# One-hots of a graph kernel's first pass built slot by slot: a single-source compare with a per-partition number in place of a two-tensor compare

## The chip, the cores and the metric

The kernel runs on one core of a Trainium2 chip. The metric is the device time of one execution in microseconds, the median over runs. The engines are named as in the profile: PE (matrix products), PEld (its weight loads), DVE (the vector engine), ACT (the scalar engine), POOL (GpSimd, which issues the row gathers here) and SP (which issues most other DMAs).

## What the reference computes

`x` holds 6250 rows of 256 numbers, `src` and `dst` the ends of 206250 edges, `edge_type_500` a type in 0..499 for each edge. Four layers follow one another, each added to `x` after a layer norm. Cut to what matters:

```python
# layer 1 (3125 nodes and 50000 edges in the original; here 6250 and 206250)
t1  = feat @ W1
msg = t1[src] + feat[src] * feat[dst] @ W2
msg = msg / (sqrt(out_deg[src]) * sqrt(out_deg[dst]))[:, None]
agg = segment_sum(msg, dst)                 # rows of edges added up per dst node
embed = where(in_cnt > 0, t1 + agg, 0) + b  # leaky_relu, then unit norm
# layer 2
x = x + layernorm(x) @ weight.T + bias
# layer 3
m = clifford_linear(h[src] * relation_emb[edge_type], msg_w, msg_b)
m = m * sigmoid(relation_emb[edge_type] @ gate_w.T + gate_b) * norm(deg[src] * deg[dst])
x = x + clifford_linear(h + segment_sum(m, dst), upd_w, upd_b)
# layer 4: gelu feed-forward of the top-k rows by a score, scaled by it
```

The edges come sorted by `dst` (there is a slow path for those that are not, which is not taken here). The kernel uses that order to cut them into windows.

## The kernel before, in words

The 6250 nodes are 49 blocks (`NB`) of 128 (`P`). Each block has 35 (`C`) tiles of 128 edge slots. The program has four stages by time:

* a prelude (to some 290 us): counts, block and window boundaries, degrees, the gate of the relations, and the table `t1_d`, also kept in three bf16 parts in SBUF (`parts_t`);
* the first pass (to some 1670 us), layers 1 and 2, with the sort of each block's edges by type;
* the second pass, layer 3, with layer 4's products beside it: gathers of 1715 tiles on POOL (L834), products on DVE (L1854), sums on PE (L958);
* the top-k and the output.

**The first pass.** It is written out by hand, step by step: every engine has a loop over the same step number `t`, 16 steps (`WINS`) to a block, with what it has to do at each step. The order on an engine is therefore fixed, and semaphores join the engines. Blocks are summed in two ways. Odd blocks gather their edges' source rows on POOL (L886, 24 blocks of 35 tiles) and sum them by one-hots (`sel1`, built by DVE at L1832) on PE at L1012. Even blocks have a count matrix instead: for each window of 8 destination nodes PE multiplies a one-hot of the source's low 7 bits (`hot_l`, 3 tiles of 128) with a one-hot of the source's block and the destination's node (`hot_r`, 392 + 294 + 147 = 833 columns for the three tiles of a window), at L985. ACT copies the counts out (L1421), and PE multiplies them with the table in three bf16 parts (L998).

DVE builds these one-hots in `edge_hots(n)`, two windows (`TWO`) at a time, 200 calls (`BATCHES`), one every four steps. The tiles hold the two windows interleaved, innermost: `hot_r` is `(n t)`, `hot_l` is `(c n t)`, and `ramp` holds 0, 0, 1, 1, 2, 2, .... A call is three compares of two tensors for `hot_r` (784, 588 and 294 elements per partition, L1818) and one for `hot_l` (768, L1821). The keys are the edges' numbers, turned to partitions by PE and copied out of PSUM to float16 by `window_keys` (L1807 and L1808).

The sort: for each block and each third of its 35 tiles (12, 12, 11), `sends(b, g)` builds `to_s` (L1943), three scaled copies `to_s3` (L1946) and `to_q`, the one-hot of the target's partition (L1948, 12 tiles of 128 in one compare of two tensors, 1536 elements). PE multiplies them at L1040 (`move`), three steps later in its own order. There is one buffer of each, so `sends` of the next third first waits for `s_sm`, PE's signal that it has read the last. `spot_q`, the targets, is written in float16 at L1930, once per three blocks. `edge_hots` has two buffers and waits for `s_h`, the histogram before last.

DVE's order in a step is: `features`, `pick_rows` (L1832), `edge_hots`, `sends`, the windows' bits and keys, `marks`, `loads3`, `totals`, `places`, then the small steps of the layer norms, each with its waits. `link(...)` is a DVE instruction on whose own completion DVE waits. Neither `edge_hots` nor the last compare of `sends` has such a link.

Of the kernel before, what the change touches and what calls it, by code (L numbers as in the profile page):

```python
# [13 lines left out]
P = 128  # L14
# [5 lines left out]
NB = -(-N // P)  # L20
# [6 lines left out]
C = 35  # L27
# [124 lines left out]
def program(nc, x, src, dst, etype, w1_0, w2_0, b_0, wf, bf, rel, msg_w, msg_b, upd_w, upd_b,  # L152
            gate_w, gate_b, wr, br, w1, b1, w2, b2, out):
    ctx = ExitStack()
    with ctx:
# [40 lines left out]
        ramp = arena[:, o:o + NODES * NB].bitcast(F16).rearrange("p (n t) -> p n t", t=TWO)  # L196
        o += NODES * NB
# [65 lines left out]
        word = arena[:, o:o + RW].bitcast(I32)  # L263
        o += RW + 1
# [4 lines left out]
        keyed_lo = arena[:, o:o + TAKE * WINS].bitcast(F16).rearrange("p (h q c w) -> p h q c w", h=2, c=TAKE, w=FOUR)  # L269
        o += TAKE * WINS  # L270
        keyed_hi = arena[:, o:o + TAKE * WINS].bitcast(F16).rearrange("p (h q c w) -> p h q c w", h=2, c=TAKE, w=FOUR)
        o += TAKE * WINS
# [22 lines left out]
        spot_q = Xf[:, o:o + RB * (C + 1)].bitcast(F16).rearrange("p (r b k) -> p r b k", r=2, k=C + 1)  # L295
        o += RB * (C + 1)
# [3 lines left out]
        to_q = Xf[:, o:o + TC4 * P // 2].bitcast(F16).rearrange("p (g q t) -> p g q t", q=P, t=TWO)  # L300
# [15 lines left out]
        hot_r = [t[:, 0:half_r].bitcast(BF16).rearrange("p (n t) -> p n t", t=TWO) for t in hots]  # L316
        hot_l = [t[:, half_r:half_r + half_l].bitcast(BF16).rearrange("p (c n t) -> p c n t", c=TAKE, t=TWO) for t in hots]
# [492 lines left out]
        def _(pool):  # L810
# [11 lines left out]
            pool.iota(ramp, [[1, NODES * NB], [0, TWO]], base=0, channel_multiplier=0,  # L822
# [72 lines left out]
        def _(pe):  # L895
            pe.wait_ge(s_const, 12)
# [444 lines left out]
        def _(act):  # L1341
# [16 lines left out]
            act.wait_ge(s_const, 12)  # L1358
# [254 lines left out]
        def _(dve):  # L1613
# [20 lines left out]
            dve.wait_ge(s_const, 12)  # L1634
# [167 lines left out]
            def window_keys(b):  # L1802

                dve.wait_ge(s_wtp, b + 1)
                lo = psE[:, 2, 0:TAKE * WINS].rearrange("p (q w c) -> p q c w", w=FOUR, c=TAKE)
                hi = psE[:, 2, TAKE * WINS:2 * TAKE * WINS].rearrange("p (q w c) -> p q c w", w=FOUR, c=TAKE)
                v.tensor_copy(keyed_lo[:, b % 2, :, :, :], lo)  # L1807
                link(v.tensor_scalar(keyed_hi[:, b % 2, :, :, :], hi, 2000.0, -2000.0, ALU.min, ALU.max))  # L1808
# [102 lines left out]
            def places(r, i):  # L1911

                b, nb = RB * r + i, blocks_of(r)
                m, first = BINS * C, C * i
                dve.wait_ge(s_rp, 2 * b + 2)
                flat = before[:, 0:m]
                mine = marked[:, i, :, :].rearrange("p c k -> p (c k)")
                link(v.tensor_tensor(flat, flat, psT[:, 0, 0:m], ALU.add))
                dve.sem_inc(s_pl, 1)
                link(v.tensor_tensor(flat, flat, mine, ALU.mult))  # L1920
                link(v.tensor_reduce(spot[:, first:first + C], flat.rearrange("p (c k) -> p k c", k=C), AX, ALU.add))
                link(v.memset(before[:, 0:1], 0.0))
# [7 lines left out]
                v.tensor_copy(spot_q[:, r % 2, 0:nb, 0:C], three(src_b[:, 0:w]))  # L1930
                link(v.tensor_copy(spot_s[:, r % 2, 0:nb, 0:C], three(src_a[:, 0:w])))

            def sends(b, g):

                n, r, i = THIRDS * b + g, b // RB, b % RB
                if n >= 1:
# [5 lines left out]
                count = lambda n: ramp[:, 0:n, :].unsqueeze(1).broadcast_to([P, m, n, TWO])  # L1942
                link(v.tensor_tensor(to_s, two(spot_s[:, r % 2, i, some]).broadcast_to([P, m, C, TWO]), count(C),  # L1943
                                     ALU.is_equal))
                for j in range(3):
                    v.tensor_tensor(to_s3[:, :, j, :, :], to_s,  # L1946
                                    two(load3[:, r % 2, j, i, some]).broadcast_to([P, m, C, TWO]), ALU.mult)
                v.tensor_tensor(to_q, two(spot_q[:, r % 2, i, some]).broadcast_to([P, m, P, TWO]),  # L1948
                                count(P), ALU.is_equal).then_inc(s_tq, 1)

            def first_pass():
                dve.wait_ge(s_part, NB)
                for t in (spot_q, spot_s):
                    v.memset(t[:, :, :, C:C + 1], 0.0)
# [343 lines left out]
```

## Time and profile before

| what | value |
|---|---|
| time, median of 3 runs | 3934.56 us (3927.07 to 3935.37) |
| span of the profiled execution | 3930.4 us |
| busy in the span: PE, DVE, POOL, ACT | 3456.7, 2831.5, 2610.6, 944.3 us |
| first pass, 325 to 1600 us: PE, DVE, POOL, ACT busy | 1193.5, 1177.6, 937.4, 483.5 us of 1275 |

The profiled execution has no time of its own in the results beside its span. It lies 4.2 us under the median and within the spread of the three runs.

Two DVE instructions with no wait between them overlap: the profile gives each its duration from start to completion, and the next starts some 0.08 us before the end of the last. What an instruction costs the engine is the distance from its start to the next one's start. It is read from the timeline, where a row with "xN" has N instructions, its start is that of the first, and its length reaches to the last one's end. Busy time counts overlapped time once. A row's shape is that of the first instruction in it.

### The profile page before, as it was taken

How to read it: one execution, taken by the hardware profiler on the slowest of the kernel's cores; microseconds unless marked ns; L12 is line 12 of the kernel's file. 1: busy time of each engine (PE TensorE's matmuls, PEld its weight loads, DVE VectorE, ACT ScalarE, POOL GpSimd, SP SyncE). 2: the span in 40 equal slices, each digit the busy share in tenths (PEclk: the TensorE clock that was granted, in tenths of full speed). 3: DMA queues.
4: the chain of work that ended last, by engine and by line, in shares of the span. 5: the costliest groups of instructions: out<-in, count | busy, mean ns of one | idle time of the engine just before them, and what ended most of it. 6: DMA issues, size and time to landing. Idle time of an engine off the chain costs nothing.

```text
span 3930.4 us, 69081 instructions
## 1 busy us (share of the span) xinstructions
PE 3456.7 (88%) x22700; PEld 2702.4 (69%) x22700; DVE 2831.5 (72%) x9160; ACT 944.3 (24%) x2408; POOL 2610.6 (66%) x2573
## 2 busy tenths in 40 slices
PE   6827999999999999778999999999999999999995
PEld 6825777777777777646776777777767777677764
DVE  8989999999999999555556556556565556656555
ACT  4042333333333434300111111111111111111111
POOL 1002777777777777367777777777777777777770
PEclk7557999999999999889999999999999999999998
DMA  5221443433443434275555555555555545555542
GB/s 154 69 88 34 111 108 108 114 107 108 109 111 106 113 107 110 81 216 135 137 135 135 135 135 136 137 135 135 136 137 134 136 133 139 136 135 133 139 129 75
DMA packets 261937, 478.46 MB, mean 122 GB/s; under 512 B 78704, under 2 KB 179072, under 8 KB 261588
## 3 DMA queue, kind: packets, MB, share of 16 engines
q0 software_dynamic: 122640, 340.29, 33.3%
q1 hardware_dynamic: 119412, 116.75, 10.2%
q10 hardware_dynamic: 19536, 17.02, 1.4%
q8 instruction: 189, 3.10, 0.3%
q14 instruction: 160, 1.31, 0.1%
HBM read 438.84 MB, written 35.00 MB: 121 GB/s over the span
## 4 chain that ended last, share of the span: by engine, by line
PE 32%; DVE 30%; POOL 20%; issue 10%; DMA 5%; ACT 2%; DVEq 0%; SPq 0%; POOLq 0%; ACTq 0%
POOL arena L834 20%; PE psE L958 6%; DMA arena<-t_d,srci 4%; PE psE L998 4%; PE psE L1012 4%; DVE relw L1818 3%; PE psE L1232 3%; DVE arena L1793 3%; DVE X L1832 2%; DVE arena L1711 2%; DVE X L1946 2%; PE psY L943 2%; PE psT L943 2%; DVE X L1948 2%; PE psE L1213 2%
## 5 line engine op out<-in xcount | busy, mean ns | idle before, releaser
L834 POOL DMA_INDIRECT arena<-t_d,srci x1715 | 1634.3, 953 | 582.2 <-issue 556.6
L886 POOL DMA_INDIRECT X<-t_d,srci x840 | 964.1, 1148 | 645.5 <-issue 450.0
L958 PE MATMUL psE<-arena 128*128 128x257 f32 x3430 | 1068.7, 393 | 79.0 <-DVE arena L1854 75.8
L1854 DVE TENSOR_TENSOR arena<-arena,psY 128x257 f32<-128x257 f32 x857 | 349.8, 420 | 437.2 <-DMA arena<-t_d,srci 235.9
L1854 DVE TENSOR_TENSOR arena<-arena,psT 128x257 f32<-128x257 f32 x858 | 349.9, 420 | 421.4 <-DMA arena<-t_d,srci 219.1
L958 PEld LDWEIGHTS psE<-arena 128*128 128x128 f32 x3430 | 541.5, 194 | 160.8 <-DVE arena L1854 84.5
L998 PE MATMUL psE<-arena,X 128*128 128x256 bf16 (+1 forms) x3675 | 535.9, 276 | 0.0
L1012 PE MATMUL psE<-X 128*128 128x257 f32 x1680 | 486.8, 383 | 8.2 <-DVE X L1832 7.7
L943 PE MATMUL psT<-relw,arena 126*128 126x257 bf16 x2574 | 434.3, 277 | 13.1 <-DVE arena L1845 13.1
L943 PE MATMUL psY<-relw,arena 126*128 126x257 bf16 x2577 | 433.1, 277 | 0.0
L998 PEld LDWEIGHTS psE<-arena,X 128*128 128x128 bf16 x3675 | 350.3, 99 | 81.6 <-issue 0.8
L1793 DVE TENSOR_SCALAR arena<-iof,dstf 128x128 f32<-128x128 f32 x1715 | 365.6, 297 | 2.9 <-PE psE L958 2.4
L943 PEld LDWEIGHTS psT<-relw,arena 126*128 126x128 bf16 x2574 | 253.2, 98 | 160.6 <-DVE arena L1845 13.7
L943 PEld LDWEIGHTS psY<-relw,arena 126*128 126x128 bf16 x2577 | 253.4, 98 | 146.5 <-issue 6.8
L1012 PEld LDWEIGHTS psE<-X 128*128 128x128 f32 x1680 | 265.0, 192 | 27.4 <-DVE X L1832 10.8
L1818 DVE TENSOR_TENSOR relw<-arena 128x784 bf16<-128x784 f16 (+2 forms) x600 | 231.3, 439 | 0.8
L1213 PE MATMUL psE<-arena 128*128 128x256 f32 (+1 forms) x800 | 189.0, 381 | 9.7 <-DVE rstd L2057 7.3
L1832 DVE TENSOR_SCALAR X<-iof,dstf 128x128 f32<-128x128 f32 x840 | 183.9, 294 | 0.9
L921 PE MATMUL psY<-arena 125*128 125x49 bf16 x1650 | 158.8, 269 | 20.8 <-DVE arena L1711 20.1
L1213 PEld LDWEIGHTS psE<-arena 128*128 128x128 f32 x800 | 145.4, 192 | 35.6 <-DVE rstd L2057 15.5
L921 PEld LDWEIGHTS psY<-arena 125*128 125x128 bf16 x1650 | 147.9, 143 | 31.6 <-DVE arena L1711 31.6
L1711 DVE TENSOR_TENSOR arena<-arena 125x3840 bf16<-125x3840 bf16 x110 | 162.5, 1536 | 3.9 <-PE psY L921 2.3
(346 smaller groups left out, 4423.1 us busy)
## 6 DMA issues: line engine op xcount, KB each, us to landing
arena<-types_d SPq DMA_DIRECT2D x245, 220.5 KB
arena<-t_d,srci POOLq DMA_INDIRECT x1715, 3.0
X<-t_d,srci POOLq DMA_INDIRECT x840
arena<-acc_d SPq DMA_DIRECT2D x98, 130.0 KB
arena<-dst_p SPq DMA_DIRECT2D x400, 1.5 KB
arena<-src_p SPq DMA_DIRECT2D x400, 1.5 KB
acc_d<-arena ACTq DMA_DIRECT2D x1, 6370.0 KB, 22.5
t_d<-arena SPq DMA_DIRECT2D x7, 910.0 KB, 4.3
```

Source lines behind the costliest of these rows:

```text
L834: pool.indirect_dma_start(gath[:, n % RG, :], None, t2_d, bass.IndirectOffsetOnAxis(ap=srci[:, n:n + 1], axis=0)).then_inc(s_g[n % RG], 16)
L886: pool.indirect_dma_start(ring1[:, n % RG1, :], None, t1_d, bass.IndirectOffsetOnAxis(ap=srci[:, at:at + 1], axis=0)).then_inc(s_g[n % RG1 ...
L921: ins = nc.tensor.matmul(psY[:, 0, 0:NB], ohlo[:, n % 2, :, t], ohhi[:, n % 2, :, t], start=(n == t == 0), stop=(n == HN - 1 and t == HG - 1))
L943: ins = nc.tensor.matmul(psR[n % BANKS][:, 0:DW], oht[0:PT, g % 2, at, :], relb[0:PT, part, c, 0:DW], start=((c, part) == (mine[0][0], 0)) ...
L958: ins = nc.tensor.matmul(psE[:, b % 2, 0:DW], sel[:, n // SG % 3, k % SG, :], gath[:, n % RG, 0:DW], start=False, stop=(k == C - 1))
L998: ins = nc.tensor.matmul(bank[:, 0:wide], adj[:, i % 2, s, :], parts_t[:, s, at0:at0 + wide], start=(s == part == 0), stop=(s == NB - 1 an ...
L1012: ins = nc.tensor.matmul(psE[:, 1, 0:DW], sel1[:, n // SG1 % 2, k % SG1, :], ring1[:, n % RG1, 0:DW], start=(k == 0), stop=(k == C - 1))
L1213: ins = nc.tensor.matmul(bank[:, i * D:i * D + many * P].rearrange("p (q n) -> p q n", n=P), f1[:, t, ht * P:ht * P + P], rows[:, t, :, :] ...
L1793: ins = v.tensor_scalar(sel[:, n % 3, i, :], iof[:, :], dstf[:, k + i:k + i + 1], None, ALU.is_equal)
L1818: v.tensor_tensor(hot_r[n % 2][:, AT[c]:AT[c + 1], :], keyed_hi[:, b % 2, j, c, first:first + TWO].unsqueeze(1).broadcast_to([P, many, TWO ...
L1832: ins = v.tensor_scalar(sel1[:, n % 2, j, :], iof[:, :], dstf[:, k + j:k + j + 1], None, ALU.is_equal)
L1854: v.tensor_tensor(rows, rows, psR[n % BANKS][:, 0:DW], ALU.mult).then_inc(s_po, 1)
```

## The change

Every one-hot of `edge_hots` and of `to_q` is now made by a compare of one tensor (the ramp, now without pairs) with a number per partition that is read from memory as float32, one instruction for each tile of 128 edges. The layouts follow: `hot_r` is `(t n)`, `hot_l` is `(t c n)`, `to_q` is `(k q)`, so that PE reads them without a stride. `keyed_lo`, `keyed_hi` and `spot_q` are float32. `to_s` still is a compare of two tensors, with a small ramp of pairs of its own (`pairs_to`), for which there is one more constant to wait for. `spot_q` and `word` have changed places in memory. A call of `edge_hots` is now 12 instructions (6 of 128 elements, 2 each of 392, 294 and 147), a block's `to_q` 35 of 128.

```diff
-        ramp = arena[:, o:o + NODES * NB].bitcast(F16).rearrange("p (n t) -> p n t", t=TWO)
+        ramp = arena[:, o:o + NODES * NB // 2].bitcast(F16)
+        pairs_to = arena[:, o:o + C + 1].bitcast(F16).rearrange("p (n t) -> p n t", t=TWO)
...
-        to_q = Xf[:, o:o + TC4 * P // 2].bitcast(F16).rearrange("p (g q t) -> p g q t", q=P, t=TWO)
+        to_q = Xf[:, o:o + TC4 * P // 2].bitcast(F16).rearrange("p (k q) -> p k q", q=P)
...
-        hot_r = [t[:, 0:half_r].bitcast(BF16).rearrange("p (n t) -> p n t", t=TWO) for t in hots]
-        hot_l = [t[:, half_r:half_r + half_l].bitcast(BF16).rearrange("p (c n t) -> p c n t", c=TAKE, t=TWO) for t in hots]
+        hot_r = [t[:, 0:half_r].bitcast(BF16).rearrange("p (t n) -> p t n", t=TWO) for t in hots]
+        hot_l = [t[:, half_r:half_r + half_l].bitcast(BF16).rearrange("p (t c n) -> p t c n", t=TWO, c=TAKE) for t in hots]
...
             def edge_hots(n):
-                b, j, first = n * TWO // WINS, n * TWO % WINS // FOUR, n * TWO % FOUR
+                b = n * TWO // WINS
                 if n >= 2:
                     dve.wait_ge(s_h, TWO * (n - 1))
-                for c, (lo, hi) in enumerate(REACH):
-                    many = (hi - lo) * NB
-                    v.tensor_tensor(hot_r[n % 2][:, AT[c]:AT[c + 1], :],
-                                    keyed_hi[:, b % 2, j, c, first:first + TWO].unsqueeze(1).broadcast_to([P, many, TWO]),
-                                    ramp[:, lo * NB:hi * NB, :], ALU.is_equal)
-                v.tensor_tensor(hot_l[n % 2][:, :, :, :],
-                                keyed_lo[:, b % 2, j, :, first:first + TWO].unsqueeze(2).broadcast_to([P, TAKE, P, TWO]),
-                                ramp[:, 0:P, :].unsqueeze(1).broadcast_to([P, TAKE, P, TWO]), ALU.is_equal).then_inc(s_r, 1)
+                for t in range(TWO):
+                    w = (n * TWO + t) % WINS
+                    for c, (lo, hi) in enumerate(REACH):
+                        v.tensor_scalar(hot_r[n % 2][:, t, AT[c]:AT[c + 1]], ramp[:, lo * NB:hi * NB],
+                                        keyed_hi[:, b % 2, w, c:c + 1], None, ALU.is_equal)
+                        ins = v.tensor_scalar(hot_l[n % 2][:, t, c, :], ramp[:, 0:P], keyed_lo[:, b % 2, w, c:c + 1], None,
+                                              ALU.is_equal)
+                ins.then_inc(s_r, 1)
...
-                v.tensor_tensor(to_q, two(spot_q[:, r % 2, i, some]).broadcast_to([P, m, P, TWO]),
-                                count(P), ALU.is_equal).then_inc(s_tq, 1)
+                for k in third(g):
+                    ins = v.tensor_scalar(to_q[:, k % TC4, :], ramp[:, 0:P], spot_q[:, r % 2, i, k:k + 1], None, ALU.is_equal)
+                ins.then_inc(s_tq, 1)
```

On DVE, early in the first pass, the order before has one call of `edge_hots` (L1818 and L1821), one of `sends` (L1943 to L1948) and the next call's start. `relw` holds the one-hots of counts, `X` those of the sort, `arena` the ramp and the keys.

```order
L1818 TENSOR_TENSOR relw<-arena 128x784
L1818 TENSOR_TENSOR relw<-arena 128x588
L1818 TENSOR_TENSOR relw<-arena 128x294
L1821 TENSOR_TENSOR relw<-arena 128x768
L1943 TENSOR_TENSOR X<-relw,arena 128x420
L1946 TENSOR_TENSOR X<-X 128x6x70 x3
L1948 TENSOR_TENSOR X<-X,arena 128x1536
```

Now the second window's half of such a call, and the same `sends` behind it; the first window's half is the same six rows once more ahead of these.

```order
L1823 TENSOR_SCALAR relw<-arena 128x392
L1825 TENSOR_SCALAR relw<-arena 128x128
L1823 TENSOR_SCALAR relw<-arena 128x294
L1825 TENSOR_SCALAR relw<-arena 128x128
L1823 TENSOR_SCALAR relw<-arena 128x147
L1825 TENSOR_SCALAR relw<-arena 128x128
L1946 TENSOR_TENSOR X<-relw,arena 128x420
L1949 TENSOR_TENSOR X<-X 128x6x70 x3
L1952 TENSOR_SCALAR X<-arena 128x128 x12
```

Nothing has changed places: four instructions have become twelve at each call, and the one of `to_q` has become twelve (eleven in a block's last third).

## Rows read from the trace of the kernel before

**Rows 1.** The page, part 1: busy us, share, instructions of each engine.
```profile
PE 3456.7 (88%) x22700; PEld 2702.4 (69%) x22700; DVE 2831.5 (72%) x9160; ACT 944.3 (24%) x2408; POOL 2610.6 (66%) x2573
```

**Rows 2.** Windows by engine: length, busy us (instructions), clock share, DMA, GB/s.
```profile
35.00:225.00 190.00, 162.40 (x1667) 150.93 (x1666) 181.12 (x169) 51.05 (x207) 0.00 (x0) 0.52 0.30 79
325.00:1600.00 1275.00, 1193.49 (x9014) 942.92 (x9013) 1177.60 (x3902) 483.53 (x1350) 937.37 (x812) 0.98 0.39 106
1600.00:1680.00 80.00, 55.29 (x312) 42.11 (x309) 34.46 (x126) 25.23 (x79) 17.09 (x18) 0.82 0.23 65
```

**Rows 3.** Waits from 325 to 1600 us: total us, times, longest us.
```profile
POOL X L886 <- PE psE L1012: 189.7, 229, 67.0
PE psY L1040 <- DVE X L1948: 41.7, 19, 3.8
PE psE L1096 <- DVE arena L2077: 16.2, 23, 1.1
DVE arena L2034 <- PE psE L998: 15.6, 9, 2.8
DVE arena L2034 <- PE psE L1012: 10.7, 9, 1.7
PE psT L985 <- DVE relw L1821: 9.9, 17, 0.8
DVE X L1943 <- PE psY L1040: 3.8, 3, 1.9
DVE arena L1918 <- PE psT L1030: 1.0, 1, 1.0
```

**Rows 4.** Timeline of DVE near 903 us: start us, length us, instructions.
```profile
901.47 0.95 DVE L1948 TENSOR_TENSOR X<-X,arena 128x1536 f16<-128x1536 f16 x1
902.34 1.06 DVE L1832 TENSOR_SCALAR X<-iof,dstf 128x128 f32<-128x128 f32 x5
903.32 1.16 DVE L1818 TENSOR_TENSOR relw<-arena 128x784 bf16<-128x784 f16 x3
904.39 0.55 DVE L1821 TENSOR_TENSOR relw<-arena 128x768 bf16<-128x768 f16 x1
904.86 0.15 DVE L2083 RECIPROCAL rstd<-rstd 128x1 f32<-128x1 f32 x1
```

**Rows 5.** DVE groups by shape, whole span: busy us, mean ns, idle before.
```profile
L1948 DVE TENSOR_TENSOR X<-X,arena 128x1536 f16<-128x1536 f16 x147 | 139.8, 951 | 0.0
L1818 DVE TENSOR_TENSOR relw<-arena 128x784 bf16<-128x784 f16 x200 | 111.7, 559 | 0.8
L1821 DVE TENSOR_TENSOR relw<-arena 128x768 bf16<-128x768 f16 x200 | 110.1, 551 | 0.0
L1818 DVE TENSOR_TENSOR relw<-arena 128x294 bf16<-128x294 f16 x200 | 60.8, 304 | 0.0
L1845 DVE TENSOR_SCALAR arena<-arena,tid 126x896 bf16<-126x896 f16 x49 | 23.0, 470 | 0.0
L1845 DVE TENSOR_SCALAR arena<-arena,tid 126x128 bf16<-126x128 f16 x52 | 13.7, 267 | 0.0
```

**Rows 6.** Timeline of DVE near 2188 us; L1845 here is 512, then 128 wide.
```profile
2188.05 0.58 DVE L1845 TENSOR_SCALAR arena<-arena,tid 126x512 bf16<-126x512 f16 x2
2188.47 0.67 DVE L1793 TENSOR_SCALAR arena<-iof,dstf 128x128 f32<-128x128 f32 x3
```

**Rows 7.** POOL's groups on the page, part 5: the gathers of both passes.
```profile
L834 POOL DMA_INDIRECT arena<-t_d,srci x1715 | 1634.3, 953 | 582.2 <-issue 556.6
L886 POOL DMA_INDIRECT X<-t_d,srci x840 | 964.1, 1148 | 645.5 <-issue 450.0
```

**Rows 8.** Timeline of the first microseconds: constants on POOL, first compare on DVE.
```profile
7.92 4.38 POOL L822 IOTA arena<- 128x784 f16 x1
13.33 0.25 DVE L1637 TENSOR_SCALAR arena<-arena 125x110 int32<-125x110 int32 x1 [10.82 <-DMA arena<-in_dst]
```

**Rows 9.** Groups of the first pass whose output the change retypes, whole span.
```profile
L1807 DVE CAST arena<-psE 128x48 f16<-128x48 f32 x25 | 5.0, 200 | 0.0
L1808 DVE TENSOR_SCALAR arena<-psE 128x48 f16<-128x48 f32 x25 | 4.9, 196 | 0.0
L1930 DVE CAST X<-arena 128x105 f16<-128x105 int32 x16 | 4.2, 265 | 0.5
```

**Rows 10.** PE's histogram and the plain products of the first pass.
```profile
L985 PE MATMUL psY<-relw 128*128 128x392 bf16 x60 | 20.4, 340 | 0.0
L998 PE MATMUL psE<-arena,X 128*128 128x257 bf16 x363 | 99.8, 275 | 0.0
L1040 PEld LDWEIGHTS psY<-X 128*128 128x128 f16 x525 | 30.7, 100 | 20.8 <-DVE X L1948 16.1
L998 PEld LDWEIGHTS psE<-arena,X 128*128 128x128 bf16 x1090 | 103.3, 99 | 23.4
```

More of the change, by code:

```diff
@@ L195, in program @@
         o = -(-(NB * TW // 2) // 2) * 2
-        ramp = arena[:, o:o + NODES * NB].bitcast(F16).rearrange("p (n t) -> p n t", t=TWO)
-        o += NODES * NB
+        ramp = arena[:, o:o + NODES * NB // 2].bitcast(F16)
+        o += NODES * NB // 2
+        pairs_to = arena[:, o:o + C + 1].bitcast(F16).rearrange("p (n t) -> p n t", t=TWO)
+        o += C + 1
         start_w = arena[:, o:o + STEPS].bitcast(I32)
@@ L262, in program @@
         o += 2 * RW
-        word = arena[:, o:o + RW].bitcast(I32)
-        o += RW + 1
+        spot_q = arena[:, o:o + 2 * RW].rearrange("p (r b k) -> p r b k", r=2, k=C)
+        o += 2 * RW + 1
         types_h = arena[:, o:o + P].bitcast(F16).rearrange("p (r e) -> p r e", r=2)
@@ L268, in program @@
         o += PAIRS * NB + 1
[L269 to L272, printed above, removed]
+        keyed_lo = arena[:, o:o + 2 * TAKE * WINS].rearrange("p (h w c) -> p h w c", h=2, c=TAKE)
+        o += 2 * TAKE * WINS
+        keyed_hi = arena[:, o:o + 2 * TAKE * WINS].rearrange("p (h w c) -> p h w c", h=2, c=TAKE)
+        o += 2 * TAKE * WINS
         marked = arena[:, o:o + BINS * RW // 2].bitcast(BF16).rearrange("p (b c k) -> p b c k", b=RB, c=BINS)
@@ L294, in program @@
         o += 2 * SG1 * P
-        spot_q = Xf[:, o:o + RB * (C + 1)].bitcast(F16).rearrange("p (r b k) -> p r b k", r=2, k=C + 1)
-        o += RB * (C + 1)
+        word = Xf[:, o:o + RW].bitcast(I32)
+        o += RW
         load3 = Xf[:, o:o + 3 * RB * (C + 1)].bitcast(F16).rearrange("p (r j b k) -> p r j b k", r=2, j=3, k=C + 1)
@@ L821, in _ @@
             pool.iota(offset, [[-NODES, WINS]], base=0, channel_multiplier=1, allow_small_or_imprecise_dtypes=True).then_inc(s_const, 1)
-            pool.iota(ramp, [[1, NODES * NB], [0, TWO]], base=0, channel_multiplier=0,
+            pool.iota(ramp, [[1, NODES * NB]], base=0, channel_multiplier=0,
+                      allow_small_or_imprecise_dtypes=True).then_inc(s_const, 1)
+            pool.iota(pairs_to, [[1, C + 1], [0, TWO]], base=0, channel_multiplier=0,
                       allow_small_or_imprecise_dtypes=True).then_inc(s_const, 1)
@@ L895, in _ @@
         def _(pe):
-            pe.wait_ge(s_const, 12)
+            pe.wait_ge(s_const, 13)
             for n in range(EN):
@@ L984, in histogram @@
                 for c, (lo, hi) in enumerate(REACH):
-                    ins = nc.tensor.matmul(bank[:, lo * NB:hi * NB], hot_l[n % 2][:, c, :, j],
-                                           hot_r[n % 2][:, AT[c]:AT[c + 1], j], start=(c == 0), stop=(c == TAKE - 1))
+                    ins = nc.tensor.matmul(bank[:, lo * NB:hi * NB], hot_l[n % 2][:, j, c, :],
+                                           hot_r[n % 2][:, j, AT[c]:AT[c + 1]], start=(c == 0), stop=(c == TAKE - 1))
                 ins.then_inc(s_h, 1)
@@ L1039, in move @@
                     i, t = k % TC4 // TWO, k % TWO
-                    ins = nc.tensor.matmul(psY[:, 0, 0:3 * C], to_q[:, i, :, t], to_s3[:, i, :, :, t],
+                    ins = nc.tensor.matmul(psY[:, 0, 0:3 * C], to_q[:, k % TC4, :], to_s3[:, i, :, :, t],
                                            start=(k == 0), stop=(k == C - 1))
@@ L1631, in _ @@
             link(v.memset(end_hi, -1.0))
-            dve.wait_ge(s_const, 12)
+            dve.wait_ge(s_const, 13)
             dve.wait_ge(s_dst, 32)
@@ L1804, in window_keys @@
                 dve.wait_ge(s_wtp, b + 1)
[L1805 to L1808, printed above, removed]
+                lo = psE[:, 2, 0:TAKE * WINS].rearrange("p (w c) -> p w c", c=TAKE)
+                hi = psE[:, 2, TAKE * WINS:2 * TAKE * WINS].rearrange("p (w c) -> p w c", c=TAKE)
+                v.tensor_copy(keyed_lo[:, b % 2, :, :], lo)
+                link(v.tensor_copy(keyed_hi[:, b % 2, :, :], hi))
                 dve.sem_inc(s_key, 1)
             def edge_hots(n):
[L1813 removed]
+                b = n * TWO // WINS
                 if n >= 2:
                     dve.wait_ge(s_h, TWO * (n - 1))
[L1816 to L1823 removed]
+                for t in range(TWO):
[6 more added lines that the diff above has]
+                ins.then_inc(s_r, 1)
             def pick_rows(n):
@@ L1929, in places @@
                 link(v.tensor_scalar(src_a[:, 0:w], src_a[:, 0:w], 7, None, ALU.logical_shift_right))
-                v.tensor_copy(spot_q[:, r % 2, 0:nb, 0:C], three(src_b[:, 0:w]))
+                v.tensor_copy(spot_q[:, r % 2, 0:nb, :], three(src_b[:, 0:w]))
                 link(v.tensor_copy(spot_s[:, r % 2, 0:nb, 0:C], three(src_a[:, 0:w])))
@@ L1941, in sends @@
                 two = lambda a: a.rearrange("p (g t) -> p g t", t=TWO).unsqueeze(2)
-                count = lambda n: ramp[:, 0:n, :].unsqueeze(1).broadcast_to([P, m, n, TWO])
-                link(v.tensor_tensor(to_s, two(spot_s[:, r % 2, i, some]).broadcast_to([P, m, C, TWO]), count(C),
-                                     ALU.is_equal))
+                link(v.tensor_tensor(to_s, two(spot_s[:, r % 2, i, some]).broadcast_to([P, m, C, TWO]),
+                                     pairs_to[:, 0:C, :].unsqueeze(1).broadcast_to([P, m, C, TWO]), ALU.is_equal))
                 for j in range(3):
@@ L1947, in sends @@
                                     two(load3[:, r % 2, j, i, some]).broadcast_to([P, m, C, TWO]), ALU.mult)
-                v.tensor_tensor(to_q, two(spot_q[:, r % 2, i, some]).broadcast_to([P, m, P, TWO]),
-                                count(P), ALU.is_equal).then_inc(s_tq, 1)
+                for k in third(g):
+                    ins = v.tensor_scalar(to_q[:, k % TC4, :], ramp[:, 0:P], spot_q[:, r % 2, i, k:k + 1], None, ALU.is_equal)
+                ins.then_inc(s_tq, 1)
             def first_pass():
                 dve.wait_ge(s_part, NB)
-                for t in (spot_q, spot_s):
-                    v.memset(t[:, :, :, C:C + 1], 0.0)
+                v.memset(spot_s[:, :, :, C:C + 1], 0.0)
                 v.memset(load3[:, :, :, :, C:C + 1], 0.0)
```

2 lines of the change are left out of this document (1 added, 1 removed).

## The prediction
> **What bounds the kernel now.** The page's busy shares come first [rows 1]: PE 88%, DVE 72%, POOL 66%. They are averages over stages, so the next view is the windows by engine. The change touches only the first pass. In its steady part, 325 to 1600 us, PE is busy 1193.5 and DVE 1177.6 of 1275 us, POOL 937.4 [rows 2]. Both PE and DVE look full, and what decides is who waits for whom there [rows 3]. DVE waits for PE in four rows: 15.6 + 10.7 + 3.8 + 1.0 = 31 us. DVE's other idle time, 97 - 31 = 66 us, is its own: it waits for the completion of its linked instructions, which a busy PE does not explain and a faster PE would not remove. PE waits for DVE longer (41.7 + 16.2 + 9.9 in the three rows shown), nearly all of its 81.5 us of idle time. So DVE sets the pace, with PE close behind. The rule for the sum follows: DVE's order is fixed by hand, so each us added to it lengthens the pass, less at most the 31 us in which it stands waiting for PE.
>
> **What an instruction costs DVE.** The timeline gives start to start [rows 4]. The three L1818 take 904.39 - 903.32 = 1.07 us and L1821 0.47 us, so a call of edge_hots is 1.54 us. L1948 takes 902.34 - 901.47 = 0.87 us, 0.08 under its duration of 951 ns [rows 5]. The rate of the two-tensor form is (559 - 304) / (784 - 294) = 0.52 ns per element [rows 5], and its fixed part 559 - 83 - 784 x 0.52 = 68 ns.
>
> The new form is not in the first pass, but the second pass has it: L1845 compares a float16 tile with a float32 number per partition and writes bf16. Its rate is (470 - 267) / (896 - 128) = 0.264 ns per element [rows 5], half of the other's. Its fixed part is larger. The pair of 512 and 128 elements takes 2188.47 - 2188.05 = 0.42 us [rows 6], so 2f + 640 x 0.264 = 420 and f = 126 ns. The float32 form L1832 agrees: five in 0.98 us is 196 ns each [rows 4], and 128 elements at twice 0.264 leave 128 ns. I take 127 ns, which makes 128, 147, 294 and 392 elements 161, 166, 205 and 230 ns. This is the center of the argument. The rate halves, but a number per partition costs some 60 ns more per instruction, and there are many more instructions.
>
> The Trainium skill speaks for the change on the rate: VectorE: DVE Perf Modes, "The perf-mode tier table", has 16-bit tensor_scalar at 4 elements a cycle and tensor_tensor at 2. The rates 0.264 and 0.52 agree. The same page of the Trainium skill, in "The TRN2 errata", prices an instruction at 58 cycles plus elements over the mode's width at 0.96 GHz. By that a 128-wide compare would be 94 ns, a call of edge_hots 1.36 for 1.51 us, a block's to_q 3.28 for 2.51, and the whole change +7 us. The rows do not bear this out: they have 161 ns, and 196 where the float32 form would be 127.
>
> **The change part by part.**
>
> * edge_hots, 200 calls. Removed: 1.54 us. Added: 2 x (230 + 205 + 166 + 3 x 161) = 2.17 us. That is +0.63 us a call and +125 us in all.
> * to_q, 49 blocks. Removed: 3 x 0.87 = 2.61 us. Added: 35 x 161 = 5.64 us. That is +3.03 us a block and +148 us in all.
> * Collisions with POOL. L1832's compares run beside POOL's gathers and still start 196 ns apart [rows 4]; the pair at L1845 gives the same fixed part within 2 ns. From no delay to 10 ns on each of 2400 + 1715 = 4115 instructions it is +0 to +41 us. I take +12, 3 ns each, nearest to the rows.
> * PE's waits give back. DVE's 31 us of waiting for PE can go, but those at L2034 are for sums that end right before them and remain in part. I take -15, between 0 and -31.
> * Retyped outputs: L1807 and L1808 write 48 elements from PSUM, L1930 105 elements, in 265 ns or less [rows 9], with the same counts per partition. The clamp of L1808 becomes a copy. One memset less. At 25 and 16 times this is under 1 us either way, and I count 0.
> * PE's reads without a stride. L985 at 392 columns takes 340 ns with its pairs interleaved, L998 at 257 contiguous columns 275 ns [rows 10]. The difference is 65 ns for 135 columns, 0.48 ns each, which is one column per cycle at 2.4 GHz and a little. Weight loads are 100 and 99 ns. The stride costs nothing now, so nothing comes back: 0.
> * The ramp: POOL's iota of 784 elements ends at 12.3 us and halves, but DVE's first compare waits for the DMA of dst until 13.3 [rows 8]: 0.
> * The added constant wait is for an iota of 72 elements in the same place, behind the same DMA: 0.
> * In the second pass nothing changes.
>
> Sum: 125 + 148 + 12 - 15 = +270 us on the profiled span of 3930.4, which is 4200. The runs' median is 4 us above that span, well inside what the terms are good for. **I predict 4200 us**, 6.8% slower. The pass would then have DVE busy in about 1450 of 1545 us and PE in 1193.5, or 77%.
>
> POOL does not become late. It issues 840 gathers at 1148 ns [rows 7], 964 us in a pass that grows by 270, and it waits 189.7 us for PE's release already [rows 3]. Even at 1.5 us a gather it would be 1260 of some 1600 us.
>
> **The rivals.**
>
> * *The one-hots off even offsets run at half rate.* A window's hot_r has 833 columns, an odd number of 2-byte elements, so the second window's tiles start 2 bytes off a word. The third tile reads the ramp from column 245, odd too. That concerns 147 + 392 + 294 + 147 = 980 of a call's 2434 elements. At L1818's rate of 0.52 they cost 0.26 us a call more, +52 us: 4252. At half that rate again it would be +155 us: 4355. Against it no row of this trace speaks, since all its 16-bit tiles start even; for it neither. The Trainium skill has the rule against this rival: Vector Engine (DVE) Microarchitecture Reference, "Performance modes", says that 4-byte alignment makes no difference. No run here shows it yet. Chance 10%.
> * *PE takes the gap badly.* With PE at 77% the granted clock can fall to the lower of its levels, 1.2 for 2.4 GHz. The rows have 0.98 at 94% busy, 0.82 at 69% in 1600 to 1680 us, and 0.52 in the prelude, where PE waits for DVE in turns [rows 2]. At a clock share of 0.85 PE's work would be 1193.5 x 0.98 / 0.85 = 1376 us, still under 1545, so most of it hides. What shows is where DVE waits for sums, L2034 and the chain of layers 1 and 2. If the 31 us of waits double instead of halving, that is +46 on my sum: 4246. Chance 8%.
> * *Not slower.* The fixed part of the new form could be smaller in this place, where twelve independent compares follow one another, than at L1845 and L1832. Without the number's 60 ns, at the 68 ns of L1818, the 4115 instructions would cost 4115 x 59 = 243 us less: 3957. The break-even of the four parts lies at 127 - 270 / 4115 us = 61 ns; under that the kernel is not slower. For it: nothing in the rows, and twelve in a row are no different from L1832's five, which already run at 196 ns. Against it: two independent readings of 126 and 128 ns. By the Trainium skill's price above the time would be 3937, on this side or next to it. Chance 3%.
> * *PE, not DVE, was the limit*, so that DVE's extra time hides. PE's idle time is 81.5 us in the pass. Were all of it slack that DVE may fill, the gain would be cut to 270 - 82 = 188: 4118. The waits above speak against it, since PE's idle time is waiting for DVE. Chance 3%.
>
> That the change doesn't do what it says is excluded by the order: twelve single-source compares stand where four two-source ones stood.
>
> **How the numbers follow.** My forecast has 76%, the rivals 10, 8, 3 and 3. Within the forecast the ends are all of the 31 us given back and no collisions (3930 + 273 - 31 = 4172), and none given back with +41 (4244). I widen to the rivals at 4252 and 4246 with room for both together, and to the low side for an f of 120 ns (-29). Range 4145 to 4290. A change within 0.2% (8 us) is what the measurement can't tell from none. Slower by more 97.5%, same 1.5%, faster 1%.
>
> **What would show it.** L1952 (to_q) at a start-to-start distance of 0.16 us, twelve in 1.93 us. A call of edge_hots at 2.17 us, with its two halves 1.09 us each; a second half that is longer is the first rival. The pass's end moves from about 1670 to 1940 us, and the second pass keeps its length. DVE idle on PE in the pass under 31 us, PE waiting for DVE by some 300 us more, mostly at L1040's and L985's successors. A clock well under 0.98 there with DVE waiting more than before is the second rival. I am wrong if the compares start 0.12 us apart or less, or if DVE's total grows as said and the span doesn't.

## The result, and the profile after

| kernel | median us | runs | ratio to before, 95% interval |
|---|---|---|---|
| before | 3933.48 (3927.07 to 3935.37) | 4 | |
| changed | 4191.91 (4189.17 to 4199.80) | 4 | 1.066 (1.0647 to 1.0673) |

The changed kernel is slower by 258 us. The forecast was 4200 us, range 4145 to 4290. Its profiled execution took 4199.8 us with a span of 4197.8, the slowest of the four, so the profiled spans are 267 us apart and the medians 258.

The page's busy times of the changed kernel:

```profile
PE 3519.8 (84%) x22700; PEld 2724.1 (65%) x22700; DVE 3119.7 (74%) x12327; ACT 936.8 (22%) x2408; POOL 2473.5 (59%) x2574
```

DVE has 3167 instructions and 288 busy us more, PE the same 22700 matmuls [rows 1]. The windows by engine show where. The first two rows are the whole first pass of before, then of the changed kernel; the last two are the second pass and the tail of each.

```profile
300.00:1640.00 1340.00, 1244.21 (x9334) 980.67 (x9335) 1219.29 (x4043) 500.28 (x1397) 954.46 (x830) 0.97 0.38 104
```
```profile
300.00:1900.00 1600.00, 1310.28 (x9347) 1006.46 (x9347) 1509.95 (x7204) 494.08 (x1399) 816.49 (x830) 0.93 0.33 87
```
```profile
1680.00:3930.00 2250.00, 2009.73 (x11469) 1541.55 (x11469) 1330.78 (x4660) 332.18 (x639) 1634.29 (x1715) 0.97 0.51 137
```
```profile
1940.00:4190.00 2250.00, 2008.96 (x11469) 1538.60 (x11469) 1329.35 (x4658) 332.17 (x639) 1637.73 (x1715) 0.97 0.52 136
```

The busy times of the second pass and the tail are the same to 4 us on every engine; the loss is in the first pass. The second pass's first gather starts at 1680.71 us before and at 1939.21 us in the changed kernel, 258.5 us later. The other 9 us between the two profiled spans are in the second pass and the tail. In the first pass DVE's busy time grows by 1509.95 - 1219.29 = 291 us. The granted clock's share (1 is 2.4 GHz, 0.5 is 1.2 GHz) falls from 0.97 to 0.93, and POOL is busy 138 us less.

The timeline of DVE in the changed kernel (start us, length us), to be read against [rows 4]: one third's to_q, and a whole call of edge_hots.

```profile
1003.05 1.90 DVE L1952 TENSOR_SCALAR X<-arena 128x128 f16<-128x128 f16 x11
1004.88 0.14 DVE L2064 TENSOR_SCALAR ssq<-ssq 128x1 f32<-128x1 f32 x1
...
1005.65 0.32 DVE L1823 TENSOR_SCALAR relw<-arena 128x392 bf16<-128x392 f16 x1
1005.88 0.25 DVE L1825 TENSOR_SCALAR relw<-arena 128x128 bf16<-128x128 f16 x1
1006.04 0.29 DVE L1823 TENSOR_SCALAR relw<-arena 128x294 bf16<-128x294 f16 x1
1006.25 0.25 DVE L1825 TENSOR_SCALAR relw<-arena 128x128 bf16<-128x128 f16 x1
1006.41 0.40 DVE L1823 TENSOR_SCALAR relw<-arena 128x147 bf16<-128x147 f16 x1
1006.59 0.26 DVE L1825 TENSOR_SCALAR relw<-arena 128x128 bf16<-128x128 f16 x1
1006.76 0.30 DVE L1823 TENSOR_SCALAR relw<-arena 128x392 bf16<-128x392 f16 x1
1006.98 0.25 DVE L1825 TENSOR_SCALAR relw<-arena 128x128 bf16<-128x128 f16 x1
1007.14 0.30 DVE L1823 TENSOR_SCALAR relw<-arena 128x294 bf16<-128x294 f16 x1
1007.36 0.24 DVE L1825 TENSOR_SCALAR relw<-arena 128x128 bf16<-128x128 f16 x1
1007.52 0.25 DVE L1823 TENSOR_SCALAR relw<-arena 128x147 bf16<-128x147 f16 x1
1007.69 0.45 DVE L1825 TENSOR_SCALAR relw<-arena 128x128 bf16<-128x128 f16 x1
1007.85 0.72 DVE L1910 TENSOR_TENSOR_SCAN arena<-ones,psT 128x280 f32<-128x280 f32 x1
```

From start to start the 128-wide compares are 0.16 us apart, the 294-wide 0.21, the 392-wide 0.23. The call takes 1007.85 - 1005.65 = 2.20 us (2.17 expected, 1.54 before), and its second half 1.09 us, no longer than its first, 1.11. Eleven of to_q take 1.83 us (11 x 0.161 = 1.77 expected).

The waits of the changed kernel's first pass, 325 to 1860 us, against [rows 3]:

```profile
POOL X L890 <- PE psE L1016: 647.0, 433, 83.8
...
PE psY L1044 <- DVE X L1952: 173.6, 70, 5.3
...
PE psT L989 <- DVE relw L1825: 53.8, 46, 1.5
...
DVE arena L2052 <- PE psE L1100: 0.3, 1, 0.3
```

The last row is the only wait of DVE for PE that is left, 0.3 us in place of 31. PE now waits for the one-hots of the sort and of the counts.

### The profile page after: what moved, and what is told of

Read it like the earlier page. It is cut to its first block, busy times and chain, and to the rows that moved or that the text cites. A ratio compares the mean times of both kernels' runs of the same rounds, so it can differ in the third digit from the quotient of the medians.

```text
span 4197.8 us, 72249 instructions
## 1 busy us (share of the span) xinstructions
PE 3519.8 (84%) x22700; PEld 2724.1 (65%) x22700; DVE 3119.7 (74%) x12327; ACT 936.8 (22%) x2408; POOL 2473.5 (59%) x2574
## 4 chain that ended last, share of the span: by engine, by line
DVE 45%; POOL 20%; PE 18%; issue 10%; DMA 5%; ACT 1%; DVEq 0%; SPq 0%; POOLq 0%; ACTq 0%
POOL arena L838 20%; DVE X L1952 7%; DVE relw L1823 6%; PE psE L962 5%; DVE relw L1825 5%; DVE X L1836 4%; DMA arena<-t_d,srci 4%; DVE X L1949 3%; PE psE L1236 3%; DVE arena L1797 3%; DVE arena L1715 2%; PE psY L925 2%; PE psY L947 2%; PE psT L947 2%; DVE X L1946 1%
## 5 line engine op out<-in xcount | busy, mean ns | idle before, releaser
L890 POOL DMA_INDIRECT X<-t_d,srci x840 | 826.2, 984 | 1045.9 <-PE psE L1016 648.2
L962 PEld LDWEIGHTS psE<-arena 128*128 128x128 f32 x3430 | 538.2, 193 | 166.2 <-DVE arena L1858 91.3
L1002 PE MATMUL psE<-arena,X 128*128 128x256 bf16 (+1 forms) x3675 | 550.8, 281 | 0.0
L1016 PE MATMUL psE<-X 128*128 128x257 f32 x1680 | 508.2, 397 | 13.3 <-DVE X L1836 13.3
L1823 DVE TENSOR_SCALAR relw<-arena 128x392 bf16<-128x392 f16 (+2 forms) x1200 | 358.8, 300 | 0.8
L1825 DVE TENSOR_SCALAR relw<-arena 128x128 bf16<-128x128 f16 x1200 | 306.5, 256 | 0.0
L1016 PEld LDWEIGHTS psE<-X 128*128 128x128 f32 x1680 | 276.4, 199 | 37.7 <-DVE X L1836 19.2
L1952 DVE TENSOR_SCALAR X<-arena 128x128 f16<-128x128 f16 x1715 | 297.5, 269 | 0.0
L1044 PE MATMUL psY<-X 128*128 128x105 f16 x1715 | 121.7, 225 | 180.3 <-DVE X L1952 179.8
L1044 PEld LDWEIGHTS psY<-X 128*128 128x128 f16 x1715 | 102.3, 105 | 223.0 <-DVE X L1952 214.7
```

What stands on the lines that cost most here:

```text
L890: pool.indirect_dma_start(ring1[:, n % RG1, :], None, t1_d, bass.IndirectOffsetOnAxis(ap=srci[:, at:at + 1], axis=0)).then_inc(s_g[n % RG1 ...
L962: ins = nc.tensor.matmul(psE[:, b % 2, 0:DW], sel[:, n // SG % 3, k % SG, :], gath[:, n % RG, 0:DW], start=False, stop=(k == C - 1))
L1002: ins = nc.tensor.matmul(bank[:, 0:wide], adj[:, i % 2, s, :], parts_t[:, s, at0:at0 + wide], start=(s == part == 0), stop=(s == NB - 1 an ...
L1016: ins = nc.tensor.matmul(psE[:, 1, 0:DW], sel1[:, n // SG1 % 2, k % SG1, :], ring1[:, n % RG1, 0:DW], start=(k == 0), stop=(k == C - 1))
L1823: v.tensor_scalar(hot_r[n % 2][:, t, AT[c]:AT[c + 1]], ramp[:, lo * NB:hi * NB], keyed_hi[:, b % 2, w, c:c + 1], None, ALU.is_equal)
L1825: ins = v.tensor_scalar(hot_l[n % 2][:, t, c, :], ramp[:, 0:P], keyed_lo[:, b % 2, w, c:c + 1], None, ALU.is_equal)
```

## The experiments

The ratio is to the kernel before as it was timed together with the experiment: 3936.5 us for e1 to e4, 3934.35 for e5 to e8, 3936.87 for e9. Differences in the text are to that, or to the changed kernel's 4191.91. Those of e4, e5 and e9 are under 2% of the time, but their intervals lie clear of 1. The edits are cut to what matters.

| kernel | median us | ratio to before, 95% interval |
|---|---|---|
| e1_hots_only | 4046.53 | 1.0281 (1.0264 to 1.0298) |
| e2_toq_only | 4060.96 | 1.0321 (1.0303 to 1.0338) |
| e3_constant_keys | 4055.87 | 1.0305 (1.0288 to 1.0322) |
| e4_before_two_parts | 3904.17 | 0.9920 (0.9903 to 0.9936) |
| e5_sel1_two_tensor | 3911.49 | 0.9940 (0.9927 to 0.9954) |
| e6_after_two_parts | 4193.49 | 1.0657 (1.0641 to 1.0673) |
| e7_float_source | 4287.88 | 1.0898 (1.0882 to 1.0915) |
| e8_both_sel_two_tensor | 4034.74 | 1.0257 (1.0242 to 1.0271) |
| e9_sel_in_two | 3979.91 | 1.0110 (1.0094 to 1.0127) |

**The two halves alone.** e1 is the changed kernel with to_q as it was (with spot_q in float16 again, a longer ramp of pairs and PE's reads with a stride, not shown):

```diff
-                for k in third(g):
-                    ins = v.tensor_scalar(to_q[:, k % TC4, :], ramp[:, 0:P], spot_q[:, r % 2, i, k:k + 1], None, ALU.is_equal)
-                ins.then_inc(s_tq, 1)
+                v.tensor_tensor(to_q, two(spot_q[:, r % 2, i, some]).broadcast_to([P, m, P, TWO]),
+                                pairs_to[:, 0:P, :].unsqueeze(1).broadcast_to([P, m, P, TWO]), ALU.is_equal).then_inc(s_tq, 1)
```

> Only edge_hots is changed to twelve single-source compares; to_q stays one compare of two tensors. Theory (DVE paces the first pass and every added us of it counts): 200 calls x 0.63 us = +125 us, less some 10 us of DVE's waits for PE: 4045 to 4060 us. Rival (PE's 82 us of idle time absorb DVE's first extra time): +45 to +80 us, 3980 to 4015.

e2 is the kernel before with only to_q changed, from a small ramp of its own without pairs (spot_q in float32 and PE's reads without a stride, not shown):

```diff
-                v.tensor_tensor(to_q, two(spot_q[:, r % 2, i, some]).broadcast_to([P, m, P, TWO]),
-                                count(P), ALU.is_equal).then_inc(s_tq, 1)
+                for k in third(g):
+                    ins = v.tensor_scalar(to_q[:, k % TC4, :], ramp1, spot_q[:, r % 2, i, k:k + 1], None, ALU.is_equal)
+                ins.then_inc(s_tq, 1)
```

> Only to_q is changed to 35 single-source compares of 128 a block; edge_hots stays as before. Theory (DVE paces): 49 x 3.03 us = +148 us, less some 10: 4070 to 4085 us. Rival (PE's idle time absorbs part): +65 to +110 us, 4000 to 4045. The two halves alone should add up to the whole, 258 us, within some 20 us by the theory; by the rival they add up to clearly less.

Measured: +110 and +124 us. The halves add up to 234, with 258 for the whole, which is 24 us apart where the theory allowed some 20. They are 15 and 24 us under the prices of 125 and 148, and e2 is 9 us under its expected range. DVE's waits for PE say why. In e1 three rows are left of them, in e2 one:

```profile
DVE arena L2037 <- PE psE L1002: 2.5, 2, 1.8
DVE X L1946 <- PE psY L1044: 1.6, 2, 1.0
...
DVE arena L2037 <- PE psE L1016: 0.3, 1, 0.3
```
```profile
DVE arena L2037 <- PE psE L1001: 2.0, 2, 1.7
```

Each half alone already takes back nearly all of the 31 us (31.1 - 4.4 = 27 in e1, 31.1 - 2.0 = 29 in e2), and the whole can take them back only once. So the two together cost 27 + 29 - 31 = 25 us more than their sum, with 24 measured. Without what came back the halves are 110 + 27 = 137 and 124 + 29 = 153 us, no less than their prices: PE's other idle time hid nothing.

**The number per partition.** e3 is the changed kernel with a constant in edge_hots. No one-hot matches it, so this kernel leaves out the even blocks' sums, while every engine still has the same instructions:

```diff
-                                        keyed_hi[:, b % 2, w, c:c + 1], None, ALU.is_equal)
+                                        -1.0, None, ALU.is_equal)
...
-                        ins = v.tensor_scalar(hot_l[n % 2][:, t, c, :], ramp[:, 0:P], keyed_lo[:, b % 2, w, c:c + 1], None,
+                        ins = v.tensor_scalar(hot_l[n % 2][:, t, c, :], ramp[:, 0:P], -1.0, None,
```

> The changed kernel, with the constant -1 in place of the number per partition in the 2400 compares of edge_hots, so that the count matrices are empty (leaves out the even blocks' sums). Theory (the number read per partition costs some 60 ns of an instruction's fixed 127): 128-wide compares start 0.10 us apart in place of 0.16, 2400 x 0.06 = -142 us: 4040 to 4060 us. Rival (the fixed part belongs to every single-source compare in its fast mode, whatever the scalar): no change, 4185 to 4200 us, distance stays 0.16.

Measured: 136 us less than the changed kernel. The timeline of e3, half a call:

```profile
1000.64 0.25 DVE L1823 TENSOR_SCALAR relw<-arena 128x392 bf16<-128x392 f16 x1
1000.81 0.19 DVE L1825 TENSOR_SCALAR relw<-arena 128x128 bf16<-128x128 f16 x1
1000.91 0.23 DVE L1823 TENSOR_SCALAR relw<-arena 128x294 bf16<-128x294 f16 x1
1001.06 0.19 DVE L1825 TENSOR_SCALAR relw<-arena 128x128 bf16<-128x128 f16 x1
1001.16 0.20 DVE L1823 TENSOR_SCALAR relw<-arena 128x147 bf16<-128x147 f16 x1
1001.27 0.19 DVE L1825 TENSOR_SCALAR relw<-arena 128x128 bf16<-128x128 f16 x1
1001.37 0.26 DVE L1823 TENSOR_SCALAR relw<-arena 128x392 bf16<-128x392 f16 x1
```

A half takes 1001.37 - 1000.64 = 0.73 us in place of 1.09 to 1.11: 0.06 us less for each of six. That is the price of reading the number per partition, shown by itself. With a constant a call is 2 x 0.73 = 1.46 us and cheaper than before's 1.54, so in edge_hots the faster rate would then have paid. In to_q it would not: 35 compares at 0.10 us are still 3.5 us for 2.61.

**The source's type.** e7 is the changed kernel with the float32 ramp `iof` in all 128-wide compares:

```diff
-                        ins = v.tensor_scalar(hot_l[n % 2][:, t, c, :], ramp[:, 0:P], keyed_lo[:, b % 2, w, c:c + 1], None,
+                        ins = v.tensor_scalar(hot_l[n % 2][:, t, c, :], iof[:, :], keyed_lo[:, b % 2, w, c:c + 1], None,
...
-                    ins = v.tensor_scalar(to_q[:, k % TC4, :], ramp[:, 0:P], spot_q[:, r % 2, i, k:k + 1], None, ALU.is_equal)
+                    ins = v.tensor_scalar(to_q[:, k % TC4, :], iof[:, :], spot_q[:, r % 2, i, k:k + 1], None, ALU.is_equal)
```

> The changed kernel, with the 2915 compares of 128 elements (hot_l and to_q) reading a float32 ramp in place of the float16 one. Theory (127 ns fixed plus elements, which take twice the time from a float32 source): the distance of starts goes from 0.162 to 0.196 us, 2915 x 0.034 = +99 us: 4280 to 4295. Rival (an instruction so short is bound by its issue, and its elements lie hidden under that): no change, 4192.

Measured: +96 us, 0.033 us for each of 2915. The elements are paid on top of the fixed part and not hidden under it. So the split into a fixed part and a rate holds in both of its terms, one moved by e3 and the other by e7.

**Who paces the pass.** e4 and e6 are the kernel before and the changed kernel with PE's products with the table's third part left out (the flag that ends a sum moves with it, not shown):

```diff
-                    for part, (at0, wide) in enumerate(((0, DW), (DW + 1, D), (DW + 1 + D, D))):
+                    for part, (at0, wide) in enumerate(((0, DW), (DW + 1, D))):
```

> The kernel before, with the table's third bf16 part left out of the even blocks' sums: PE has 1225 matmuls of 256 columns less, some 130 us of its work. Theory (DVE paces, PE only in the 31 us that DVE waits for it): -10 to -31 us, 3900 to 3925 us. Rival (PE paces the pass, or shares the pace evenly with DVE): -60 us or more, under 3875.

> The changed kernel, with the table's third bf16 part left out of the even blocks' sums, as was done to the kernel before (there -32 us). Theory (DVE alone paces the changed first pass, PE has slack and the lower granted clock costs nothing): 0 to -6 us, 4185 to 4193. Rival (PE's lower clock share of 0.93 is part of the added time): -15 us or more, under 4177.

Measured: -32 us from before, and +2 us from the changed kernel, which is nothing. The profiled spans of before and e4 are 27 us apart. DVE's waits for PE went from 31 to 4 us, and more than half of what e4 keeps is this row:

```profile
DVE arena L2034 <- PE psE L998: 2.2, 2, 1.7
```

e4's time lies in its range, but the 32 us are 1 more than the whole 31 that was its end; the waits account for 27. The windows by engine of e6 settle the clock as well:

```profile
325.00:1860.00 1535.00, 1186.54 (x7873) 880.06 (x7874) 1469.10 (x7000) 474.81 (x1349) 800.02 (x812) 0.89 0.32 88
```

PE has 1186 matmuls fewer than in the changed kernel there and an even lower clock share, 0.89, and the time is the same. A lower clock on an engine that waits costs nothing here.

**The change turned round.** If a number per partition costs 60 ns an instruction, then the place to use that is where the kernel already pays it. e5 is the kernel before with sel1's five float32 compares made one of two tensors:

```diff
-                for j in range(SG1):
-                    ins = v.tensor_scalar(sel1[:, n % 2, j, :], iof[:, :], dstf[:, k + j:k + j + 1], None, ALU.is_equal)
-                ins.then_inc(s_sel, 1)
+                v.tensor_tensor(sel1[:, n % 2, :, :], dstf[:, k:k + SG1].unsqueeze(2).broadcast_to([P, SG1, P]),
+                                iof[:, :].unsqueeze(1).broadcast_to([P, SG1, P]), ALU.is_equal).then_inc(s_sel, 1)
```

> The kernel before, with the change turned round at another place: sel1's five float32 single-source compares (0.98 us) become one compare of two tensors of 640 elements. Theory (the fixed part per instruction decides; float32 with two tensors runs at one element per cycle, 1.04 ns, fixed 68 ns): 0.73 us, 168 times 0.25 us less = -41 us of DVE's work; PE and the end of the chain let some 25 to 41 us through: 3893 to 3912 us, faster than both kernels. Rival (the mode's rate decides, halving it can't win): same or slower, 3935 or more.

Measured: 23 us (0.6%) faster than before, 280 us faster than the changed kernel, and the fastest here of those that leave nothing out. The instruction costs 0.73 us, as expected, start to start:

```profile
902.34 0.82 DVE L1831 TENSOR_TENSOR X<-dstf,iof 128x640 f32<-128x640 f32 x1
903.07 1.16 DVE L1818 TENSOR_TENSOR relw<-arena 128x784 bf16<-128x784 f16 x3
```

The time lies at the upper end of the expected 3893 to 3912 us; as a difference, 23 us are 2 less than the 25 expected. Of the 41 us saved, DVE's waits for PE take back 14:

```profile
DVE arena L2033 <- PE psE L998: 19.0, 9, 3.0
DVE arena L2033 <- PE psE L1012: 17.2, 11, 2.0
...
DVE X L1942 <- PE psY L1040: 7.1, 11, 2.1
...
DVE arena L1917 <- PE psT L1030: 1.4, 1, 1.4
```

They sum to 44.7 us, from 31.1. PE waits for DVE 40.5 + 8.8 + 8.1 = 57 us in its three largest rows, from 68. So the two are now nearer to being equal limits.

e8 does the same to the second pass's `sel` too (seven compares become one of 896 elements, `sel[:, n % 3, :, :]` from `dstf[:, k:k + SG]`).

> As the kernel before with sel1 made by one two-tensor compare, and the second pass's sel too (seven compares in 1.37 us become one of 896 elements, some 1.00 us, 245 times). Theory (the second pass is not paced by DVE, which is busy 59% of it): DVE has 90 us less to do there and the time stays that of the sel1 kernel within 10 us, 3885 to 3912. Rival (products queue behind these compares on DVE, and PE waits for products): up to 40 us less than the sel1 kernel, under 3875.

Both theories failed: it is 123 us slower than e5. DVE did save its time, and the second pass grew. POOL's gathers of the second pass took 1023 ns, with 953 before [rows 7]:

```profile
L834 POOL DMA_INDIRECT arena<-t_d,srci x1715 | 1753.6, 1023 | 581.3 <-issue 559.3
```

Their busy time is up 1753.6 - 1634.3 = 119 us, and that is the loss: the gathers, with some 0.3 us between them, pace the second pass. DVE's own waits there turn from PE to the gathers' DMA.

The mean of 1023 ns hides two kinds. In e8 143 of the 1715 gathers take over 1.3 us, 1.80 in the mean, and each of them meets an 896-wide compare; those under 1.1 us take 0.95 in the mean. In e5 none takes over 1.3. One such meeting in e8's timeline:

```profile
2165.88 1.08 DVE L1792 TENSOR_TENSOR arena<-dstf,iof 128x896 f32<-128x896 f32 x1
2165.93 1.85 POOL L834 DMA_INDIRECT arena<-t_d,srci  x1 [0.30 <-issue]
```

The gather ends 2167.78 - 2166.96 = 0.82 us after the compare. So do all 168 gathers of e8 that start at least 0.02 us after such a compare and at least 0.15 us before its end, within 0.01 us. It is as if such a gather stood until the compare's end, and then needed all but some 0.13 us of its own 0.95. e9 splits the compare in two (sel1 is as in e5):

```diff
+                for i, j in ((0, 4), (4, SG)):
+                    ins = v.tensor_tensor(sel[:, n % 3, i:j, :], dstf[:, k + i:k + j].unsqueeze(2).broadcast_to([P, j - i, P]),
+                                          iof[:, :].unsqueeze(1).broadcast_to([P, j - i, P]), ALU.is_equal)
```

> As the kernel with both sel tiles made by two-tensor compares, but the second pass's 896-wide one split in two, of 512 and 384 elements (start to start some 0.60 and 0.47 us in place of 1.00). The 896-wide form had lengthened POOL's gathers of the second pass from 953 to 1023 ns, which is the +120 us of that pass. Theory (a gather that meets such a compare stands until its end, so the loss goes with the square of its length): 0.60^2 + 0.47^2 over 1.00^2 is 0.58, +70 us on the sel1 kernel: 3970 to 3990, gathers at some 993 ns. Rival (the loss goes with the total time of such compares, 1.07 us a group): +128 us: 4030 to 4045, gathers at some 1027 ns.

Measured: +68 us on e5, with 70 expected, and the gathers at 993 ns:

```profile
L834 POOL DMA_INDIRECT arena<-t_d,srci x1715 | 1703.5, 993 | 581.2 <-issue 563.0
```

The total time of such compares has risen and the loss has nearly halved, so the total time does not decide. The square law is not shown by it, though the number came out. The law has the number of meetings fall with the length too. In the trace nearly as many gathers take over 1.3 us, 134 for 143, all at a 512-wide compare, and each loses less: 1.47 us in the mean for 1.80. What the trace bears out is the other half of the theory, that a gather that meets a compare stands until its end.

## Why the prediction was right, point by point

* *DVE paces the first pass.* Right, shown by e4 and e6: 1225 matmuls less give 32 us before and nothing after. DVE's other idle time, 66 us before, is its own, as I had it: the changed kernel has 69 us (1466 us busy of 1535, 325 to 1860), with no wait for PE in it but 0.3 us. One reading was loose: the three rows of PE waiting for DVE are 67.8 of its 81.5 us of idle time, not nearly all.
* *edge_hots +125 us and to_q +148 us.* Right. The distances are those worked out, 0.16, 0.21 and 0.23 us; a call is 2.20 us for 2.17. DVE's busy time in the pass grew by 291 us, with 273 for the two terms. The 18 us over are 4 ns for each of 4115 instructions, where I had taken 3 for collisions with POOL. That they are collisions is not shown.
* *A fixed part of 127 ns, some 60 of it for the number per partition.* Right, shown by e3 with 0.06 us. e5, from the other side, agrees: one compare of 640 elements took 0.73 us for the five's 0.98.
* *DVE's waits give back 15 us.* This term was mis-sized: all 31 came back, already at half of the change. I had argued that L2034 waits for sums that end right before it, and that part of this would remain. In the changed kernel DVE has no wait for a sum at that line any more (now L2037). With 291 - 31 = 260 us the account closes on the first pass's 258.5 and on the 258 between the medians. Against the forecast's 270, the terms of price and collisions were 6 us too small and the waits' term gave back 16 too little; the first hid part of the second. That the profiled execution, the slowest of the four, took 4199.8 us is luck; the median is 8 us under the forecast.
* *Compares at odd offsets at half rate (10%).* Excluded by the trace of the changed kernel. The second half of a call, which writes at odd offsets, takes 1.09 us for the first's 1.11, and over the trace the medians of the halves are 1.10 and 1.10 us. The 147-wide compares, which read from an odd column in both halves, take 0.17 to 0.18 us for 0.166. The Trainium skill's rule in Vector Engine (DVE) Microarchitecture Reference, "Performance modes", that 4-byte alignment makes no difference, agrees.
* *PE takes the gap badly (8%).* The clock share did fall, to 0.93 and not to the rival's 0.85, and it cost nothing (e6). One of the signs that I gave came out otherwise by it: PE was idle 290 us of 1600, with 96 of 1340 before. That is 194 us more and not some 300, because its busy time grew by 66 us at the lower share.
* *Not slower (3%).* The break-even needed a fixed part of 61 ns. With a constant it is near that, some 100 - 34 = 66 ns by e3, with a number per partition it is not. The Trainium skill's price in VectorE: DVE Perf Modes, "The TRN2 errata", gives an estimate of 94 ns for a 128-wide compare at four elements a cycle. That agrees with e3's 0.10 us and not with the 0.16 us that count here; for the two-tensor form it gives 469 ns at 784 elements, with 477 measured. The measured 60 ns between 0.10 and 0.16, times 4115, are 247 us, nearly the whole result.
* *POOL does not become late.* Right: its gathers of the first pass even became shorter, 984 ns for 1148, which was not foreseen (below).

## What to carry to other kernels

Price a vector instruction by its distance from start to start in two parts, fixed and per element, and count instructions before modes: here twice the rate lost to 60 ns for a per-partition number, because most of the tiles had 128 elements. By an estimate from these rows, two windows in one compare of two tensors (68 + 1.04 m ns for m elements each) beat two single-source compares (254 + 0.53 m) up to some 360 elements a window. Where another engine waits, first find out for how much of its time the pacing engine waits in turn; that amount comes back once, at the first part of a change. Before making instructions longer, look at what paces the stage: the same kind of edit won 23 us where DVE paced and lost 123 where POOL's gathers did.

## What the runs showed of the hardware that was not expected

POOL's gathers depend on what DVE runs beside them. In the first pass the 840 gathers take 1148 ns in the mean before, 1090 in e2, 995 in e1 and 984 in the changed kernel, where twelve short single-source compares stand for four long ones of two SBUF tensors; in the second pass the same 1715 take 953 to 955 in all four. The page's row of the changed kernel, against L886 in [rows 7]:

```profile
L890 POOL DMA_INDIRECT X<-t_d,srci x840 | 826.2, 984 | 1045.9 <-PE psE L1016 648.2
```

POOL gained 138 us of busy time there and waited it away, since it did not pace that pass. I had expected a small loss from collisions.

It is not the two-tensor form alone that holds a gather. The kernel before has single-source compares as long as 0.45 us in the second pass (L1845), and this is one of them with a gather that meets it:

```profile
2987.82 0.45 DVE L1845 TENSOR_SCALAR arena<-arena,tid 126x896 bf16<-126x896 f16 x1
2987.97 1.11 POOL L834 DMA_INDIRECT arena<-t_d,srci  x1 [0.30 <-issue]
```

The gather ends 2989.08 - 2988.27 = 0.81 us after this compare too. Of the compares at L1845 that take 0.33 us or more, 16 have a gather that starts 0.075 to 0.24 us into them, and all 16 gathers end 0.81 to 0.83 us after the compare, as in e8. So in these traces both forms hold a gather, and what it loses is what is left of the compare, less some 0.13 us. Compares of 0.16 to 0.23 us from start to start leave little of that, which fits the 984 ns. The mean alone tells less, because it also depends on how many gathers happen to start inside a compare: with sel1 as one 640-wide compare in place of five, e5's first pass has 1123 ns, less than the 1148 before. Why gathers that start in the first hundredths of a microsecond of a compare are often not held is open.
